# A fused transformer kernel: where the covariance steps issue their gathers, and where VectorE sums the gathered blocks

## The reference, cut to what matters

```python
x = x + _L0_attn_a_ref(_layernorm(x, axis=-1), ...)      # layer 0, rope
x = x + _L0_ffn_ref(_layernorm(x, axis=-1), ...)         # layer 1, ffn
x = x + _L0_attn_b_ref(_layernorm(x, axis=-1), ...)      # layer 2, cov
x = x + _L0_ffn_ref(_layernorm(x, axis=-1), ...)         # layer 3, ffn
...
# moe_ff, the end of layers 1 and 3: each token takes its two experts' outputs
    h = jax.nn.gelu(t @ w1[e] + b1[e]) @ w2[e] + b2[e]
    out = out + we[:, None] * h
...
# _L0_attn_b_ref, layer 2 (d is the head size, 8)
q_c = q - q.mean(axis=-1, keepdims=True)
k_c = k - k.mean(axis=-1, keepdims=True)
cov = jnp.einsum('bhqd,bhkd->bhqk', q_c, k_c) / d
q_var = (q_c * q_c).sum(axis=-1, keepdims=True) / (d - 1)
k_var = (k_c * k_c).sum(axis=-1, keepdims=True) / (d - 1)
var = jnp.einsum('bhqo,bhko->bhqk', q_var, k_var) / d
attn = jax.nn.softmax(cov + var, axis=-1)
out = jnp.einsum('bhqk,bhkd->bhqd', attn, v)
```

## Time and profile before

| | |
|---|---|
| Median of three runs | 831.25 us (830.76 to 831.65) |
| Profiled execution, own time | 825.84 us |
| Profiled execution, span | 824.0 us |
| Mean granted TensorE clock | 0.952 |
| Busy: PE, DVE, ACT, POOL | 724.6, 540.3, 535.1, 483.1 us |
| Chain that ended last, by engine | PE 52%, DVE 19%, POOL 14%, issue 8% |

### The profile page before, as it was taken

How to read it: one execution, slowest core, us unless ns; L and a number is a source line. 1 busy time by engine, 2 the same in 40 slices (tenths; PEclk the granted TensorE clock), 3 DMA queues, 4 the chain that set the end, 5 groups by cost and what they waited for, 6 DMA issues and landing times.

```text
span 824.0 us, 21303 instructions
## 1 busy us (share of the span) xinstructions
PE 724.6 (88%) x7166; PEld 547.9 (66%) x7166; DVE 540.3 (66%) x1370; ACT 535.1 (65%) x1264; POOL 483.1 (59%) x906
## 2 busy tenths in 40 slices
PE   1999999999999969989887998999999996999960
PEld 1765665666676559989865565666666654899950
DVE  5689999888989623112576888888888973311222
ACT  0277777787887737646546667777878873865630
POOL 6657778877754561505755665865686357060536
PEclk9789999999999979999989999999999997999985
DMA  9400000000000245667110000000000015486832
GB/s 274 144 2 3 2 4 3 3 3 3 3 4 3 69 138 155 205 182 216 54 35 14 15 18 8 3 3 3 3 4 3 3 35 162 126 231 180 256 91 70
DMA packets 57657, 56.29 MB, mean 68 GB/s; under 512 B 6856, under 2 KB 42448, under 8 KB 57552
## 3 DMA queue, kind: packets, MB, share of 16 engines
q1 hardware_dynamic: 39200, 39.13, 16.7%
q0 software_dynamic: 4096, 8.40, 3.4%
q10 hardware_dynamic: 14256, 7.41, 3.1%
HBM read 40.10 MB, written 14.29 MB: 66 GB/s over the span
## 4 chain that ended last, share of the span: by engine, by line
PE 52%; DVE 19%; POOL 14%; issue 8%; DMA 3%; ACT 2%; SPq 0%; ACTq 0%; POOLq 0%; DVEq 0%
DVE M L1110 11%; PE bankR L727 9%; PE bankE L714 9%; PE bankO L477 8%; PE bankE L450 7%; PE bankE L496 6%; PE bankR L463 4%; POOL Yg L1601 2%; POOL sorted_u L1581 2%; PE bankE L702 1%; DVE X L1343 1%; PE bankR L517 1%; POOL R L1475 1%; PE bankE L487 1%; POOL Zhl L1458 1%
## 5 line engine op out<-in xcount | busy, mean ns | idle before, releaser
L1110 DVE TENSOR_REDUCE M<-bankR 128x2 f32<-128x512 f32 x512 | 326.9, 684 | 58.8 <-PE bankR L463 56.0
L839 ACT ACTIVATE Pr<-bankE 128x512 f32<-128x512 f32 x512 | 275.9, 594 | 101.8 <-PE bankE L450 101.2
L463 PE MATMUL bankR<-KQ 32*128 32x256 f32 x1024 | 168.7, 336 | 13.5 <-DVE M L1110 5.5
L477 PE MATMUL bankO<-Pr,Vx 128*32 128x256 f32 x2048 | 139.2, 389 | 2.3 <-ACT OT L833 1.3
L450 PE MATMUL bankE<-KQ 32*128 32x256 f32 x1024 | 139.7, 331 | 1.3 <-ACT Pr L839 1.1
L450 PEld LDWEIGHTS bankE<-KQ 32*128 32x128 f32 x1024 | 85.4, 186 | 78.0 <-issue 46.2
L1332 DVE COPY Yb<-bankR 128x128 f32<-128x128 f32 x92 | 26.8, 291 | 156.3 <-PE bankR L727 150.2
L463 PEld LDWEIGHTS bankR<-KQ 32*128 32x128 f32 x1024 | 104.0, 189 | 31.1 <-DVE M L1110 25.8
L952 ACT ACTIVATE G<-bankE,W 128x128 f32<-128x128 f32 x368 | 101.0, 378 | 20.3 <-PE bankE L714 19.6
L1581 POOL DMA_INDIRECT sorted_u<-U,SLOT x64 | 62.3, 974 | 82.4 <-DVE past L1312 43.1
L1601 POOL DMA_INDIRECT Yg<-sorted_y,SLOT x64 | 62.1, 970 | 81.5 <-DVE Yb L1332 57.8
(11 more groups left out here) (169 smaller groups left out, 1089.3 us busy)
## 6 DMA issues: line engine op xcount, KB each, us to landing
W<-in_w1b SPq DMA_DIRECT2D x92, 258.0 KB, 3.2
sorted_y<-Yb ACTq DMA_DIRECT2D x92, 64.0 KB
XT<-sorted_u SPq DMA_DIRECT2D x20, 256.0 KB, 2.9
sorted_u<-Yg SPq DMA_DIRECT2D x2, 1472.0 KB, 9.9
KQ<-MT SPq DMA_DIRECT2D x128, 4.0 KB
X<-in_x SPq DMA_DIRECT2D x8, 128.0 KB, 7.2
sorted_u<-U,SLOT POOLq DMA_INDIRECT x64
Yg<-sorted_y,SLOT POOLq DMA_INDIRECT x64, 2.6
```

Of the source, the lines that this page charges most:

```text
L463: k = mm(dve_bank("raw", layer, b, h)[:, z * T:z * T + T], QT[rows, kb, g, z * P:z * P + P], KT[rows, kb, g, :], start=True, stop=True)
L477: k = mm(bankO[SL * j:SL * j + SL, cols], Vx[:, b % VB, kc, HG * g + j, :], Pr[:, g % 2, j, kc, :], start=(g % 2 == 0 and kc == 0), stop=( ...
L839: nc.scalar.activation(Pr[:, (h // HG) % 2, h % HG], act_bank("S", layer, b, h).rearrange("p (k q) -> p k q", k=TT), ACT.Exp, scale=EXP_SC ...
L1110: v.tensor_reduce(M[:, b % 2, :, h], dve_bank("raw", layer, b, h).rearrange("p (t k) -> p t k", t=TT), AX.X, ALU.max, negate=True).then_in ...
```

## The change

Three things move; no instruction is added or taken away.

1. GpSimd, steps 4 to 6 and step 3: one gather goes between the stacked keys and their squares (inside `stack_k`), and the other three go behind `norm`. Before, one stood ahead of the keys, one behind the squares, one behind the values, one behind `norm`. Steps 1 and 2 keep the old places (`filling`).
2. GpSimd, step 3 (`FILL`): `norm` of block 3 goes to the head of the step, ahead of the stacks of block 2.
3. VectorE, steps 4 to 7: `combine` and the statistics of a late block stand ahead of `do_max(m, 3)`, not behind `do_max(m, 4)`.

```diff
--- before.py
+++ after.py
@@ -1183,6 +1183,9 @@
                     do_fold()
                 if ranking(a):
                     count_tiles(a[0] // 2, 0)
+                if late(p):
+                    combine(0, p[1])
+                    norm_in(*p)
                 if m:
                     do_max(*m, 3)
                 if rope:
@@ -1195,9 +1198,6 @@
                     rotate(*n, 0, 1)
                 if ranking(a):
                     name_experts(a[0] // 2, 0)
-                if late(p):
-                    combine(0, p[1])
-                    norm_in(*p)
                 if nxt and not late(nxt):
                     norm_in(*nxt)
                 if u:
@@ -1478,7 +1478,7 @@
                 src = R1[:].rearrange("p c t h x -> p c t (h x)") if kind == "rope" else QKV
                 return src[:, c].rearrange("p t (h x) -> p (t h) x", x=HD)
 
-            def stack_k(layer, b):
+            def stack_k(layer, b, beside=None):
                 kind, ev = LAYERS[layer], stacked
                 k = 0
                 if kind != "rope":
@@ -1493,6 +1493,8 @@
                               twice(kv)).then_inc(ev.sem, 1)
                 need(pool, ev, layer, b, k + 1)
                 g.tensor_tensor(ks[:, :, HD:2 * HD], kv, as32(ks[:, :, 0:HD]), ALU.subtract).then_inc(ev.sem, 1)
+                if beside:
+                    gather(*beside)
                 if kind == "cov":
                     need(pool, squared, layer, b)
                     hk = hsq[:, STH:2 * STH].unsqueeze(2)
@@ -1628,31 +1630,34 @@
                 pool.wait_ge(ready_pool, 8)
 
             def step(u, t, a, m, n, p):
-                early = p and turned_ahead(p)
-                if early and p:
+                early = p and (turned_ahead(p) or p == (2, FILL))
+                if early:
                     norm(*p)
-                fetched = p and p[0] == 2 and 0 < p[1] < NB - 1
+                filling = p and p[0] == 2 and 0 < p[1] < FILL
+                fetched = p and p[0] == 2 and FILL <= p[1] < NB - 1
                 if u:
                     close(*u)
-                if fetched:
+                if filling:
                     gather(0, p[1] + 1, range(0, 1))
                 if n:
                     if n == (3, 0):
                         clear_cov()
-                    stack_k(*n)
-                if fetched:
+                    stack_k(*n, (0, p[1] + 1, range(0, 1)) if fetched else None)
+                if filling:
                     gather(0, p[1] + 1, range(1, 2))
                 if t:
                     unrope(*t)
                 if n:
                     stack_q(*n)
                     stack_v(*n)
-                if fetched:
+                if filling:
                     gather(0, p[1] + 1, range(2, 3))
                 if p and not early:
                     norm(*p)
+                if filling:
+                    gather(0, p[1] + 1, range(3, 4))
                 if fetched:
-                    gather(0, p[1] + 1, range(3, 4))
+                    gather(0, p[1] + 1, range(1, 4))
 
             for ph in range(2):
                 for s in range(STEPS):
```

## The result

The changed kernel takes 836.49 us (median of 12 runs, 832.34 to 839.14) against 831.57 before (12 runs, 828.38 to 833.91): a ratio of 1.0066, 95% interval 1.0046 to 1.0086. It is slower, by about 5 us. The forecast was no change, 831.5, with a range up to 834.5; the rival on the slow side (a clock fall in each step, 833.9) had 0.15.

The account below looks back on a forecast made before the run. A VectorE, GpSimd, TensorE chain was taken to bound steps 4 to 7. The profiled 825.84 us, less 4.49 (head of step 4), plus 2.35 (hold) and 2.38 (clock), gave 826.1, or 831.5 as median; range 827.5 to 834.5.

Parts of the forecast that it names:

- the rival on the slow side: Steps 4 to 7: a clock fall in each of the four steps, 833.9 us; chance 0.15.
- What bounds a step and the new hold: Steps 4 to 7: a VectorE, GpSimd, TensorE chain ends last; afterwards TensorE is held at head 9, about 2.3 us.
- Rival 3: Steps 4 to 7: head 9 doesn't hold TensorE, steps of 16.0 us, 12.6 us gained, 818.6 us; chance 0.14.
- The head of step 4: Start of step 4: block 3's earlier normalising ends TensorE's wait, first maximum at 443.33 and not 447.82, 4.49 us gained.
- The step's sum: Steps 4 to 7, first maximum to next: five terms and 0.5 us less stall make 18.62 us, together 2.35 us lost.
- Sums and statistics: VectorE, ahead of head 6's maxima in steps 4 to 7: four sums and the statistics take 2.26 us.
- head 9's weights to the next transposes: TensorE's dense stretch in steps 4 to 7: 7.15 us, less 0.5 of stall that goes, 6.65 us.
- The clock: TensorE behind the new hold in steps 4 to 7: two clock falls in four steps, 1.19 us each, 2.38 us lost.

Follow-up runs that it names:

- e2: Only the VectorE part, sums and statistics ahead of the maxima of heads 6 to 9, on the kernel before: 843.24 us, ratio 1.0104.
- e3: The changed kernel with sums and statistics between the maxima of heads 7 and 8, not ahead of head 6: 824.67 us, ratio 0.9911.
- e4: The kernel before with one edit, block 3 of layer 2 normalised at the head of GpSimd's step 3: 832.35 us, ratio 0.9986.
- e7: The kernel before with only the early normalising of block 3, the same kernel as e4 run again: 829.81 us, ratio 0.9970.
- e13: The kernel before with the new gather places alone, no early normalising and no moved sums: 826.23 us, ratio 0.9942.
- e5: The changed kernel with head 8's raw scores computed ten times over in steps 4 to 7: 833.41 us, ratio 1.0038.
- e1: Only the GpSimd part of the change on the kernel before, sums and statistics back behind the later maxima: 825.46 us, ratio 0.9930.

## Why the prediction was wrong

**What bounds a step and the new hold: right.** The wait for Zhl went, head 6's maximum releases head 9, and GpSimd was ready 4.9 us early. Rival 3, head 9 free, is out (e2, e3).

**The head of step 4: right in the trace, 4.4 us for 4.49,** but worth 1 to 2.5 us in the median when it stands alone (e4, e7), and most of it comes with the gathers' new places anyhow: step 3 to 4 takes 21.50 us before, 18.7 in e13 and 17.75 with both. I had priced it from one execution and passed it on whole. What I had not asked is what the clock does with the rest of the phase once a stall goes.

**The step's sum: right in three of five terms.** 6.75, 0.72 and 2.23 us came as written (6.74, 0.74, 2.23). Where the clock holds, head 9's weights to the next transposes took 6.2 (453.03 to 459.22 in e5) for my 6.65, 0.45 less. **Sums and statistics were mis-sized: 2.93 us and not 2.26.** I took their time from the place they left. At the new place they run beside GpSimd's query copies. The Trainium skill ("GPSIMD Engine Reference", section "Key points") says that GpSimd shares its SBUF interfaces with VectorE, with contention where a VectorE instruction has two SBUF inputs; a sum reads Yg and X. The traces agree: single sums take 337 to 704 ns there and 341 to 427 before, and four together 2.28 us. The less of them lies beside the copies, the shorter they are: 2.02 us in steps 5 and 6 of e2, where the copies begin 1.2 us into the sums, 1.60 in e3, where only the copies of hsq and V are left, 1.51 in e1, where the copies are through. Step 4 of e2 doesn't fit, 2.76 us with the copies as late as in its steps 5 and 6, so something else takes part. No run moved the copies alone, and that it is the shared interface is the page's account. It makes 2.7 us in four steps; with the shorter stretch the step comes to 18.85 for my 18.62.

**The clock: the step that failed.** I took two falls at 1.19 us, 2.4 in all. There were four, in both profiles, at 1.7 to 2.1 in the first: 7.5 us. I had counted falls from three single stalls elsewhere, though this hold recurs behind the same stretch in each step, and I had priced one by the K transposes up to P·V alone, from a low stretch of 3.5 us (492.0 to 495.5). The low stretch lasted 7 us here and took head 9, P·V and what lay between with it. My price held where the stretch was short: 1.2 us in steps 5 and 6 of e5. With the steps' 3.3 us without a fall (four of 18.85 against 72.13) in place of my 2.35, and the 4.4 gained, the sum comes to 6.3 us slower where I had 0.24; the medians say 4.9.

The rival built on four falls had the right count and was too cheap, 833.9. It leaned on the Trainium skill ("TensorE: Matmul & The Clock Gate", section "HAM oscillation — how this bites in real kernels"), where a wait in every tile has every tile start at the low clock. This case's traces agree in the count, four of four. But the page tells it of DMA waits of some 3 to 5 us, and I had put my stall at 2.3 us (it was 2.96), so the page alone didn't decide it. And three falls came in e5, where all but 0.80 us of the hold was filled.

## What to carry to other kernels

Before moving work ahead of something in one engine's queue, follow each buffer that the displaced instructions free to the instruction that takes it next, and read what stands behind that one on its engine; one pair of maxima later (e3) the same move gained. Price a moved instruction at its new neighbours, and a stall that recurs with the clock at its low level in every step, for all of the path behind it. And price from several executions: one trace had the kernel before 5 us under its median.

Ask, too, what a move removes elsewhere. e3's order gains because sums one pair sooner bring the statistics, and with them Zhl, in time for TensorE (e1 still waits 1.0 us a step for it), at the price of a hold of only 0.65 us.

## What the runs showed that I had not expected

The spread of this kernel, 825 to 840 us on unchanged code, goes in part with the mean granted clock: of 100 runs of the kernel before the 25 fastest average a clock of 0.954, the 25 slowest 0.945.
